# An attention and expert block: the values product of a group in one run, and a router with the experts held still in four column quarters

## The chip, the cores and the metric

The kernel runs on one core of a Trainium2 chip. The metric is the device time of one execution in microseconds (us). A core has the engines TensorE (PE in the rows; its weight loads are PEld), VectorE (DVE), ScalarE (ACT), GpSimd (POOL) and SyncE (SP, which issues DMAs); each works through its own list of instructions in order, and they wait for each other by semaphores. PSUM has eight banks of 128 partitions x 512 float32.

## The reference

x is (16, 512, 1024), ctx (16, 512, 256). 16 heads of 64 are in 4 groups of 4; the heads of a group share one key and one value slice, and keys and values are both ctx.

```
scores = layernorm(x) @ ctx.T / 8, per head and its group's slice      # 512 x 512
out    = softmax(scores) @ v                                       # v = ctx
x      = x + out.reshape(b, s, 1024) @ Wc.T + bc
h      = layernorm(x)
logits = h @ gate_kernel                                           # 1024 -> 32 experts
top 8 of softmax(logits), renormalised
x      = x + sum over the 8 experts of weight * down(silu(gate(h)) * up(h))
```

## The kernel before, in words

One program does a setup (transposed output weights in a high and a low part), an attention stage (attention, projection, second layernorm, router, choice of experts and the table of their rows), a short schedule, and the experts stage. The change touches setup and attention only.

**The attention stage** goes over 64 tiles of 128 rows, four tiles (s = 0 to 3) to each of 16 batches b. The batches between the first and the last run in a hardware loop, four tiles to a pass, so each engine comes to the loop's end once per batch. Within a tile every engine runs over the heads h = 0 to 15 in the same way: `tile(t)` issues what is due at head h, in the order in which it is written. That order is fixed by hand in a set of dictionaries that name, for each kind of work, the heads at which it is issued. Work of several tiles is interleaved: while attention of tile i runs, the projection belongs to tile i-1, the second layernorm's transposes, router and choice to tile i-2, the ranks and table writes to tile i-3, and the first layernorm and queries to tile i+1.

**TensorE at head h of tile i**, in order: scores of head h+3 (lines 798 and 799, into one of two S banks; waits for the exponent of head h+1), the four transposes of the probabilities of head h (line 813), half a block of the values product at odd heads (line 836), key transposes for the next batch at four heads of tiles 3 and 0 (`KEYS`, line 785), the ranks at head 1 (lines 885, 886), chunks of the projection (`PROJECT`, line 855), the transposes of the second layernorm's rows at heads 4 and 5 (line 871), the router at head 6 (line 877), and a quarter of the next tile's query transposes at heads 10 to 13 (line 776; they all use one bank, so each waits until ScalarE has copied the one before, line 460).

**Values** (`values`, line 836). For a group of four heads, and each of four chunks c of 128 context rows, two products: the stationary operand is the value chunk, 128x64, and the moving one the transposed probabilities of two heads, 256 columns. The two go to column halves 0-63 and 64-127 of the array and to the partition halves of one O bank. A float32 product is two passes on the array. The block of a group (8 products, 16 passes) is issued in two halves: chunks 0 and 1 at the head 4g+1, chunks 2 and 3 at 4g+3, one group later than its probabilities.

**Projection** (`project`). A chunk c is three float32r products of 512 columns, with the stationary operands oT_hi, oT_hi and oT_lo. `PROJECT` maps a head to (back, n, c0, c1): half n of tile i-back, chunks c0 to c1. After an odd chunk of half n = 1 TensorE signals `out_read`, since oT_hi and oT_lo of that group may then be overwritten. The part that waits for it is not touched by the change:

```
OUT_NORM = {0: (1, 2), 4: (1, 3), 8: (0, 0), 12: (0, 1)}                          # L216
OUT_SPLIT = {h + 1: back_group for h, back_group in OUT_NORM.items()}
def split_out_hi(i, g):                                                           # ScalarE, L490
    act.wait_ge(onorm_ready, G * i + g + 1)
    if g < G - 1:
        wait(act, out_read, (G - 1) * (i - 1) + g + 1)
    act.activation(oT_hi[:, 2 * g:2 * g + 2, :], o_norm[:, :, :], ACT.Copy).then_inc(othi_ready, 1)
```

ScalarE issues it (line 496) at head 9 for group 0 of the running tile, and VectorE's `split_out_lo` (line 621) waits for it at the same head.

**ScalarE at head h**, in order: the copy of the transposed probabilities of head h (line 487; VectorE has those of heads 1, 5, 9, 13, line 607), the exponent of head h+3 (line 479), `split_out_hi`, values and keys of the next batch (`keys_hi`, lines 471, 472), `normalise2` at head 3 (line 502), copies of its transposes at 4 and 5 (line 509), `normalise1` of the next tile at 6 (line 448), the high part of its queries at 7 (line 455), `top_exponent` at 8 (line 515), query copies at 10 to 13.

**VectorE at head h**: the maximum of head h+3 (line 592), inverses at 2, 6, 10, 14, its probability copies, the output's normalisation and low part, ranks at 2, statistics at 1, 2, 11 and 15, the table entries at 3 and 5, the logits and the choice of experts at 7, halves of the residual at 8 and 15. **POOL**: both layernorms' factors, the low part of the queries (line 393) at head 7, the bias addition (line 399) at 8, and eight table scatters (line 411).

**Router** (`router`, line 877): for each of eight chunks of 128 features, xn2T[:, c] (128x128) is stationary and gate_sb[:, c] (128x32) moves; all eight add up in one bank. VectorE copies the 32 logits of each row at head 7, and the second half of the projection, which uses the same bank, waits for that copy.

Of the kernel before, what the change touches and what calls it, by code (L numbers as in the profile page):

```python
# [16 lines left out]
F32 = mybir.dt.float32  # L17
# [7 lines left out]
P = 128  # L25
# [31 lines left out]
def moe_block(nc, x, ctx_in, Wc, bc, gate_w, gate_proj, up_proj, down_proj, out):  # L57
# [36 lines left out]
    with top:  # L94
        def sb(ctx, name, shape, dt):
            return ctx.enter_context(nc.sbuf_tensor(name, shape, dt))
# [11 lines left out]
        with attention_mem:  # L108
# [4 lines left out]
            ones_bf = sb(attention_mem, "ones_bf", [P, P], BF16)  # L113
            gate_sb = sb(attention_mem, "gate_sb", [P, DC, E], F32)
            bias_row = sb(attention_mem, "bias_row", [P, D], F32)
            iota_e = sb(attention_mem, "iota_e", [P, E], F32)
            token_id = sb(attention_mem, "token_id", [P, 1], F32)

            setup_stage(nc, sb, sem, banks, Wc, bc, gate_w, xn_dram, table, out, ident, ident_r, before_bf,
                        ones_bf, gate_sb, bias_row, iota_e, token_id, slot_base, expert_base, WcT_hi, WcT_lo,  # L120
                        D=D, DC=DC, E=E, T=T, TABLE_ROWS=TABLE_ROWS)
# [31 lines left out]
            FACTOR_STEPS = 2 + 2 * NEWTON_STEPS  # L153
            ROOT_SEED = float(0x5f3759df)
            logits = sb(attention_mem, "logits", [P, E], F32)
            top_v = sb(attention_mem, "top_v", [P, TOP_K], F32)
# [40 lines left out]
            ln2_chain = sem("ln2_chain")  # L197
            pool2_chain, ln2_ready, xn2_ready = sem("pool2_chain"), sem("ln2_ready"), sem("xn2_ready")
            xt2_done, xt2_copied, router_done, logits_copied = sem("xt2_done"), sem("xt2_copied"), sem("router_done"), sem("logits_copied")
            top_ready, topexp_ready, chosen_ready, rank_done = sem("top_ready"), sem("topexp_ready"), sem("chosen_ready"), sem("rank_done")  # L200
            rank_copied, entry_ready = sem("rank_copied"), sem("entry_ready")
            fence = {n: sem(f"fence_{n}") for n in ("dve", "pool", "sp")}

            BACK_STEPS = 12


# [11 lines left out]
            DVE_HEAD = 1  # L218
            VALUE_CHUNKS = {1: (0, 1), 3: (2, 3)}

            PROJECT = {0: (1, 0, 1, 2), 1: (1, 0, 2, 3), 2: (1, 0, 3, 4), 3: (1, 0, 4, 5), 4: (1, 0, 5, 6), 7: (1, 0, 6, 8),
                       8: (1, 1, 0, 2), 9: (1, 1, 2, 3), 10: (1, 1, 3, 4), 11: (1, 1, 4, 5), 12: (1, 1, 5, 6), 13: (1, 1, 6, 7),
                       14: (1, 1, 7, 8), 15: (0, 0, 0, 1)}
            NEXT_STATS, NEXT_FACTORS, NEXT_NORM, NEXT_SPLIT, NEXT_QUERIES, NEXT_BIAS = (1, 2), 2, 6, 7, (10, 11, 12, 13), 8
            RESIDUAL, STATS2 = (8, 15), (11, 15)
            FACTORS2, NORM2, TRANSPOSE2, ROUTER, CHOOSE, MARK, TOP_EXP = 0, 3, (4, 5), 6, 7, (11, 13), 8
            RANKS, TAKE_RANKS, PLACE, ENTER = 1, 2, 3, 5
# [216 lines left out]
            def _(act):  # L444
# [60 lines left out]
                def copy_xn2(j, n):  # L505
                    act.wait_ge(xt2_done, 2 * j + n + 1)
                    if n == 0:
                        wait(act, router_done, j)
                    act.activation(xn2T[:, 4 * n:4 * n + 4, :], turned(j, n)[:, :].rearrange("p (c t) -> p c t", c=4),
                                   ACT.Copy).then_inc(xt2_copied, 1)  # L510

                def top_exponent(j):
                    act.wait_ge(top_ready, j + 1)
                    wait(act, entry_ready, j)
                    act.activation(top_e[:, :], top_v[:, :], ACT.Exp, bias=neg_top[:, :], accum_out=top_s[:, :]
                                   ).then_inc(topexp_ready, 1)

                def tile(t):
                    i = t.i
                    for h in range(H):  # L520
# [14 lines left out]
                        if h in TRANSPOSE2 and t.back2:  # L535
                            copy_xn2(i - 2, TRANSPOSE2.index(h))
                        if h == NEXT_NORM and t.next:
                            normalise1(i + 1, t.next_s)
# [20 lines left out]
                for j in (LAST - 1, LAST):  # L559
                    normalise2(j)  # L560
                    for n in range(2):
                        copy_xn2(j, n)
                    top_exponent(j)

# [199 lines left out]
            def _(pe):  # L764
# [109 lines left out]
                def router(j):  # L874
                    pe.wait_ge(xt2_copied, 2 * j + 2)
                    for c in range(DC):
                        last = nc.tensor.matmul(turned(j, 0)[:, 0:E], xn2T[:, c, :], gate_sb[:, c, :], start=(c == 0), stop=(c == DC - 1))
                    last.then_inc(router_done, 1)

# [9 lines left out]
                def tile(t):  # L889
                    i = t.i  # L890
                    for h in range(H):
# [20 lines left out]
                        if h == ROUTER and t.back2:  # L912
                            router(i - 2)
                        if h in NEXT_QUERIES and t.next:
                            transpose_queries(i + 1, NEXT_QUERIES.index(h))
# [16 lines left out]
                for j in (LAST - 1, LAST):  # L932
                    for n in range(2):
                        transpose_xn2(j, n)
                    router(j)
                    ranks(j)

# [7 lines left out]

def setup_stage(nc, sb, sem, banks, Wc, bc, gate_w, xn_dram, table, out, ident, ident_r, before_bf, ones_bf, gate_sb,
                bias_row, iota_e, token_id, slot_base, expert_base, WcT_hi, WcT_lo, *, D, DC, E, T, TABLE_ROWS):
# [4 lines left out]
    with mem:  # L952
# [46 lines left out]
        def _(dve):  # L999
            dve.memset(zeros[:, :], 0.0).then_inc(empty_made, 1)  # L1000
            dve.memset(empty[:, :, 1], 0)
            dve.wait_ge(ident_made, 1)
            dve.tensor_copy(ident_r[:, :], ident[:, :]).then_inc(ident_r_made, 1)
            dve.wait_ge(made, 4)

# [654 lines left out]
```

## Time and profile before

| | us |
|---|---|
| median of 3 runs | 9428.77 (9426.17 to 9434.4) |
| the profiled execution | 9434.62 |
| its span, first to last instruction | 9432.9 |

| engine | busy us | share of the span |
|---|---|---|
| TensorE, products | 9123.3 | 97% |
| TensorE, weight loads | 7523.7 | 80% |
| VectorE | 5856.4 | 62% |
| POOL | 5063.9 | 54% |
| ScalarE | 4224.1 | 45% |

The shares are means over stages with different limits. The attention stage takes some 2669 us of the span, the experts stage nearly all the rest. Weight loads overlap with products, so the two lines of TensorE don't add up. The ends of products are modelled in the profile; distances between starts are the better measure of what one costs.

### The profile page before, as it was taken

How to read it: one execution, taken by the hardware profiler on the slowest of the kernel's cores; microseconds unless marked ns; L12 is line 12 of the kernel's file. 1: busy time of each engine (PE TensorE's matmuls, PEld its weight loads, DVE VectorE, ACT ScalarE, POOL GpSimd, SP SyncE). 2: the span in 40 equal slices, each digit the busy share in tenths (PEclk: the TensorE clock that was granted, in tenths of full speed). 3: DMA queues.
4: the chain of work that ended last, by engine and by line, in shares of the span. 5: the costliest groups of instructions: out<-in, count | busy, mean ns of one | idle time of the engine just before them, and what ended most of it. 6: DMA issues, size and time to landing. Idle time of an engine off the chain costs nothing.

```text
span 9432.9 us, 173987 instructions
## 1 busy us (share of the span) xinstructions
PE 9123.3 (97%) x46640; PEld 7523.7 (80%) x46641; DVE 5856.4 (62%) x9216; ACT 4224.1 (45%) x7010; POOL 5063.9 (54%) x4825
## 2 busy tenths in 40 slices
PE   8999999999969999999999999999999999999999
PEld 5777777777747888888888888888888888888888
DVE  5666666666645656666556666566666656656565
ACT  6666666666633333333333333333333333333333
POOL 2444444444445655666555566556665556555564
PEclk9999999999979999999999999999999999999999
DMA  2221212112124555555455555455555455555554
GB/s 96 60 57 59 63 53 63 57 55 64 56 62 106 119 109 113 115 128 127 107 108 110 111 133 119 105 113 113 114 117 119 106 125 107 119 107 111 125 115 81
DMA packets 723597, 926.17 MB, mean 98 GB/s; under 512 B 405521, under 2 KB 536593, under 8 KB 723090
## 3 DMA queue, kind: packets, MB, share of 16 engines
q0 software_dynamic: 209920, 604.72, 30.0%
q1 hardware_dynamic: 513298, 316.84, 13.0%
q8 instruction: 184, 3.01, 0.1%
q14 instruction: 195, 1.60, 0.1%
HBM read 1073.17 MB, written 376.45 MB: 154 GB/s over the span
## 4 chain that ended last, share of the span: by engine, by line
PE 61%; DMA 3%; issue 2%; DVE 2%; SPq 1%; ACT 1%; POOL 0%; DVEq 0%; ACTq 0%; POOLq 0%
PE bank L1569 40%; PE bank L1592 21%; DMA gu_raw<-in_L_ffn_up_proj 3%; SPq L1304 1%; DVE gu_lo L1483 0%; ACT xT_hi L1396 0%; ACT gu_hi L1403 0%; DVE xT L1472 0%; DVE h L1495 0%; DVE h_lo L1500 0%; DVE d_lo L1488 0%; DVE xT_lo L1477 0%; DVE h_hi L1498 0%; POOL xg L1356 0%; DVEq L41 0%
## 5 line engine op out<-in xcount | busy, mean ns | idle before, releaser
L1356 POOL DMA_INDIRECT xg<-xn_rows,gather_row x2304 | 2753.7, 1195 | 2076.9 <-PE bank L1569 1300.9
L1569 PE MATMUL bank<-xT_hi,gu_hi 128*128 128x512 f32 (+2 forms) x6912 | 2553.0, 369 | 106.4 <-DVE xT_lo L1477 95.9
L1569 PE MATMUL bank<-xT_lo,gu_hi 128*128 128x512 f32 (+2 forms) x6912 | 2543.1, 368 | 0.0
L1569 PE MATMUL bank<-xT_hi,gu_lo 128*128 128x512 f32 (+2 forms) x6912 | 2543.0, 368 | 0.0
L1414 ACT ACTIVATE gated<-bank 128x512 f32<-128x512 f32 x432 | 258.3, 598 | 3034.4 <-PE bank L1569 2681.5
L1569 PEld LDWEIGHTS bank<-xT_hi,gu_hi 128*128 128x128 f32 x6912 | 1299.1, 188 | 282.3 <-issue 94.9
L1368 POOL DMA_INDIRECT out_rows<-rows_out,entry_now x576 | 1139.0, 1977 | 678.3 <-DVE rows_out L1507 324.8
L1569 PEld LDWEIGHTS bank<-xT_lo,gu_hi 128*128 128x128 f32 x6912 | 1299.4, 188 | 159.3 <-issue 0.5
L1569 PEld LDWEIGHTS bank<-xT_hi,gu_lo 128*128 128x128 f32 x6912 | 1298.9, 188 | 158.8
L1592 PE MATMUL bank<-d_hi,h_hi 128*128 128x512 f32 x3162 | 1255.9, 397 | 70.1 <-DVE h_lo L1500 70.1
L1495 DVE TENSOR_TENSOR h<-bank,gated 128x512 f32<-128x512 f32 x432 | 297.6, 689 | 1580.9 <-ACT gated L1414 1195.1
L1592 PE MATMUL bank<-d_lo,h_hi 128*128 128x512 f32 x3162 | 1244.4, 394 | 0.0
L1592 PE MATMUL bank<-d_hi,h_lo 128*128 128x512 f32 x3162 | 1242.8, 393 | 0.0
L1483 DVE TENSOR_TENSOR gu_lo<-gu_raw,gu_hi 128x2048 fp32r<-128x2048 f32 x432 | 973.6, 2281 | 246.0 <-ACT gu_hi L1403 130.5
L592 DVE TENSOR_REDUCE neg_max<-bank 128x1 f32<-128x512 f32 x1024 | 704.4, 688 | 566.8 <-PE bank L799 464.2
L1403 ACT ACTIVATE gu_hi<-gu_raw 128x2048 fp32r<-128x2048 f32 x432 | 809.2, 1907 | 179.1 <-DMA gu_raw<-in_L_ffn_up_proj 165.4
L411 POOL DMA_INDIRECT slot_table<-entry,slot_i x512 | 507.9, 992 | 706.2 <-ACT pT L487 532.5
L479 ACT ACTIVATE probs<-bank,neg_max 128x512 f32<-128x512 f32 x1024 | 701.8, 685 | 344.1 <-DVE neg_max L592 307.4
L1507 DVE TENSOR_SCALAR rows_out<-bank,entry_now 128x512 f32<-128x512 f32 x576 | 431.3, 749 | 676.4 <-PE bank L1592 657.0
L1421 ACT ACTIVATE rows_out<-bank,entry_now 128x512 f32<-128x512 f32 x576 | 395.1, 686 | 1000.3 <-PE bank L1592 865.7
L1592 PEld LDWEIGHTS bank<-d_hi,h_hi 128*128 128x128 f32 x3162 | 600.8, 190 | 243.1 <-issue 122.6
L1472 DVE STREAM_TRANSPOSE xT<-xg 128x512 f32<-128x512 f32 x1152 | 747.3, 687 | 0.0
(159 smaller groups left out, 13150.0 us busy)
## 6 DMA issues: line engine op xcount, KB each, us to landing
gu_raw<-in_L_ffn_gate_proj SPq DMA_DIRECT2D x576, 384.0 KB
gu_raw<-in_L_ffn_up_proj SPq DMA_DIRECT2D x576, 384.0 KB
d_raw<-in_L_ffn_down_proj SPq DMA_DIRECT2D x144, 1536.0 KB
xg<-xn_rows,gather_row POOLq DMA_INDIRECT x2304
x_t<-in_x SPq DMA_DIRECT2D x64, 512.0 KB, 4.8
inv_wide<-inverse_sums SPq DMA_DIRECT2D x512, 64.0 KB
out_rows<-x SPq DMA_DIRECT2D x64, 512.0 KB, 5.5
xn_rows<-xn SPq DMA_DIRECT2D x64, 512.0 KB
```

The costliest lines, as they stand in the source:

```text
L411: pool.indirect_dma_start(out=table, out_offset=bass.IndirectOffsetOnAxis(ap=slot_i[:, k:k + 1], axis=0), in_=entry[:, k, :], in_offset=No ...
L479: act.activation(probs[h % 4][:, :], S_BANK[h % 2][:, :], ACT.Exp, bias=neg_max[:, h:h + 1], accum_out=row_sum[:, h:h + 1]).then_inc(exp_r ...
L592: dve.tensor_reduce(neg_max[:, h:h + 1], S_BANK[h % 2][:, :], AX.X, ALU.max, negate=True).then_inc(max_ready, 1)
L1356: pool.indirect_dma_start(out=xg[:, m, :], out_offset=None, in_=quarter_rows, in_offset=bass.IndirectOffsetOnAxis(ap=gather_row[:, m:m + 1 ...
L1368: pool.indirect_dma_start(out=out, out_offset=bass.IndirectOffsetOnAxis(ap=entry_now[:, q, 0:1], axis=0), in_=rows_out[:, q, :], in_offset ...
L1403: act.activation(gu_hi[:, :, :, cols], gu_raw[:, :, :, cols].rearrange("p n c m -> p c n m"), ACT.Copy).then_inc(guhi_ready, 1)
L1421: act.activation(rows_out[:, q, 0:512], D_BANK[q][0][:, :], ACT.Copy, scale=entry_now[:, q, 1:2].bitcast(F32)).then_inc(left_ready, 1)
L1472: dve.transpose(xT[:, :, 2 * pair * QUAD:2 * (pair + 1) * QUAD].rearrange("p c (m r) -> p m c r", r=QUAD), xg[:, 2 * pair:2 * pair + 2, :] ...
L1483: dve.tensor_tensor(gu_lo[:, :, :, cols], gu_raw[:, :, :, cols].rearrange("p n c m -> p c n m"), gu_hi[:, :, :, cols].bitcast(F32), ALU.su ...
L1507: dve.tensor_scalar(rows_out[:, q, 512:1024], D_BANK[q][1][:, :], entry_now[:, q, 1:2].bitcast(F32), None, ALU.mult).then_inc(right_ready, 1)
L1569: last = nc.tensor.matmul(bank[:, 0:cols], w[:, c, n, j * P:(j + 1) * P], v[:, c, 0:cols], start=(c == 0 and w is gu_hi and v is xT_hi), s ...
L1592: last = nc.tensor.matmul(D_BANK[q][n][:, 0:cols], v[:, k, q * P:(q + 1) * P], w[:, k, n * 512:n * 512 + cols], start=(k == ks[0] == 0 and ...
```

## The change

- The values block of a group is issued whole, at head 4g+1: `VALUE_CHUNKS` goes from {1: (0, 1), 3: (2, 3)} to {1: (0, 1, 2, 3)}.
- The chunks of the projection are laid on other heads, so that none shares a head with values.
- The router holds gate_sb[:, c] (128x32) still and moves xn2T[:, c] (128 columns). Chunk c goes to the column quarter c % 4, so that four partial sums of 32 experts x 128 rows stand in four partition quarters of a bank. ScalarE copies them (`copy_parts`, head 6), and one float32 product at head 7, with the copy stationary and a 128x32 matrix of ones in the right places moving (`fold`, made once in the setup), adds the quarters and turns the result back to rows x experts.

```diff
+            dve.tensor_reduce(fold[:, :], ident[:, :].rearrange("p (j e) -> p e j", e=E), AX.X, ALU.add)
...
-            VALUE_CHUNKS = {1: (0, 1), 3: (2, 3)}
-
-            PROJECT = {0: (1, 0, 1, 2), 1: (1, 0, 2, 3), 2: (1, 0, 3, 4), 3: (1, 0, 4, 5), 4: (1, 0, 5, 6), 7: (1, 0, 6, 8),
-                       8: (1, 1, 0, 2), 9: (1, 1, 2, 3), 10: (1, 1, 3, 4), 11: (1, 1, 4, 5), 12: (1, 1, 5, 6), 13: (1, 1, 6, 7),
-                       14: (1, 1, 7, 8), 15: (0, 0, 0, 1)}
+            VALUE_CHUNKS = {1: (0, 1, 2, 3)}
+
+            PROJECT = {0: (1, 0, 1, 2), 2: (1, 0, 2, 4), 3: (1, 0, 4, 5), 4: (1, 0, 5, 6), 6: (1, 0, 6, 7), 7: (1, 0, 7, 8),
+                       8: (1, 1, 0, 1), 10: (1, 1, 1, 3), 11: (1, 1, 3, 4), 12: (1, 1, 4, 6), 14: (1, 1, 6, 8), 15: (0, 0, 0, 1)}
...
-            FACTORS2, NORM2, TRANSPOSE2, ROUTER, CHOOSE, MARK, TOP_EXP = 0, 3, (4, 5), 6, 7, (11, 13), 8
+            FACTORS2, NORM2, TRANSPOSE2, ROUTER, FOLD, CHOOSE, MARK, TOP_EXP = 0, 3, (4, 5), 6, 7, 7, (11, 13), 8
...
+                def copy_parts(j):
+                    act.wait_ge(parts_done, j + 1)
+                    wait(act, router_done, j)
+                    act.activation(parts[:, :], turned(j, 0)[:, 0:P], ACT.Copy).then_inc(parts_copied, 1)
...
+                        if h == ROUTER and t.back2:
+                            copy_parts(i - 2)
                         if h == NEXT_NORM and t.next:
                             normalise1(i + 1, t.next_s)
...
                     for c in range(DC):
-                        last = nc.tensor.matmul(turned(j, 0)[:, 0:E], xn2T[:, c, :], gate_sb[:, c, :], start=(c == 0), stop=(c == DC - 1))
-                    last.then_inc(router_done, 1)
+                        rows = slice(E * (c % EXPERT_SETS), E * (c % EXPERT_SETS + 1))
+                        last = nc.tensor.matmul(turned(j, 0)[rows, 0:P], gate_sb[:, c, :], xn2T[:, c, :],
+                                                start=(c < EXPERT_SETS), stop=(c >= DC - EXPERT_SETS))
+                    last.then_inc(parts_done, 1)
+
+                def fold_parts(j):
+
+                    pe.wait_ge(parts_copied, j + 1)
+                    nc.tensor.matmul(turned(j, 0)[:, 0:E], parts[:, :], fold[:, :], start=True, stop=True).then_inc(router_done, 1)
...
+                        if h == FOLD and t.back2:
+                            fold_parts(i - 2)
```

## Rows read from the trace of the kernel before

**Rows 1.** The page, part 1: busy time of each engine over the whole span.
```profile
PE 9123.3 (97%) x46640; PEld 7523.7 (80%) x46641; DVE 5856.4 (62%) x9216; ACT 4224.1 (45%) x7010; POOL 5063.9 (54%) x4825
```

**Rows 2.** Windows: stretch, length, busy time (instructions) by engine, granted clock, DMA share, GB/s.
```profile
921.50:961.00 39.50, 39.50 (x251) 29.32 (x250) 26.10 (x61) 26.32 (x60) 18.18 (x31) 1.00 0.19 54
44.00:2713.00 2669.00, 2588.04 (x16210) 1912.32 (x16211) 1751.33 (x3932) 1774.21 (x3960) 1137.25 (x1879) 0.99 0.20 57
2217.10:2220.50 3.40, 3.40 (x13) 3.03 (x12) 2.14 (x6) 2.00 (x6) 0.00 (x0) 0.50 0.01 2
```

**Rows 3.** Timeline, a second tile, TensorE: start, length, instruction; heads 1 to 3.
```profile
921.51 0.39 PE L798 MATMUL bank<-kT,qT 128*128 128x512 f32 x1
...
922.50 1.08 PE L836 MATMUL bank<-pT,v 128*64 128x256 f32 x8
...
924.36 0.39 PE L798 MATMUL bank<-kT,qT 128*128 128x512 f32 x1
...
925.96 0.40 PE L798 MATMUL bank<-kT,qT 128*128 128x512 f32 x1
```

**Rows 4.** The same tile, TensorE: the router in head 6, and head 7.
```profile
934.23 1.91 PE L877 MATMUL bank<-gate_sb,xn2T 128*128 128x32 f32 x16
935.98 0.48 PE L798 MATMUL bank<-kT,qT 128*128 128x512 f32 x1
```

**Rows 5.** The same tile: a maximum in head 2, xn2, and its transposes in head 4.
```profile
925.02 0.69 DVE L592 TENSOR_REDUCE neg_max<-bank 128x1 f32<-128x512 f32 x1
...
928.95 1.23 ACT L502 ACTIVATE xn<-x,ln 128x1024 f32<-128x1024 f32 x1
...
930.38 0.60 PE L871 MATMUL bank<-ident,xn 128*128 128x128 f32 x4
```

**Rows 6.** The same tile: head 6 begins, normalise1, a short exponent, the bias addition.
```profile
933.24 0.48 PE L798 MATMUL bank<-kT,qT 128*128 128x512 f32 x1
...
936.13 1.23 ACT L448 ACTIVATE xn<-x_t,ln 128x1024 f32<-128x1024 f32 x1
...
941.86 0.30 ACT L515 ACTIVATE top_e<-top_v,neg_top 128x8 f32<-128x8 f32 x1
...
943.21 2.40 POOL L399 TENSOR_TENSOR x_t<-x_t,bias_row 128x1024 f32<-128x1024 f32 x1
```

**Rows 7.** The same tile: both splits, heads 10 and 11, the next head 1.
```profile
943.96 0.41 ACT L496 ACTIVATE oT_hi<-o_norm 128x256 fp32r<-128x256 f32 x1
...
944.40 1.50 DVE L621 TENSOR_TENSOR oT_lo<-o_norm,oT_hi 128x256 fp32r<-128x256 f32 x1 [0.55 <-ACT oT_hi L496]
...
944.71 0.39 PE L798 MATMUL bank<-kT,qT 128*128 128x512 f32 x1
...
945.83 0.68 DVE L592 TENSOR_REDUCE neg_max<-bank 128x1 f32<-128x512 f32 x1
...
947.22 0.59 ACT L460 ACTIVATE qT<-bank 128x512 fp32r<-128x512 f32 x1
...
949.48 0.46 PE L776 MATMUL bank<-ident_r,xq 128*128 128x128 f32 x4
...
961.02 0.39 PE L798 MATMUL bank<-kT,qT 128*128 128x512 f32 x1
```

**Rows 8.** Line 621 in this stage: count, ns min/median/max, first and last start, forms.
```profile
L621 DVE TENSOR_TENSOR oT_lo<-o_norm,oT_hi x252: 415/426/2703, 105.5 to 2699.2; 128x256 fp32r<-128x256 f32 x126
```

**Rows 9.** Timeline at a turn of a batch: head 14 begins; the standstill; head 2.
```profile
2203.38 0.47 PE L798 MATMUL bank<-kT,qT 128*128 128x512 f32 x1
...
2215.02 0.69 DVE L592 TENSOR_REDUCE neg_max<-bank 128x1 f32<-128x512 f32 x1 [4.88 <-issue]
...
2216.57 0.50 PE L798 MATMUL bank<-kT,qT 128*128 128x512 f32 x1 [2.98 <-ACT probs L479]
```

**Rows 10.** Timeline, a fourth tile, ScalarE: exponent of head 13, first query copy.
```profile
2194.56 0.69 ACT L479 ACTIVATE probs<-bank,neg_max 128x512 f32<-128x512 f32 x1 [0.16 <-DVE neg_max L592]
...
2196.46 0.60 ACT L460 ACTIVATE qT<-bank 128x512 fp32r<-128x512 f32 x1
```

More of the change, by code:

```diff
@@ L114, in moe_block @@
             gate_sb = sb(attention_mem, "gate_sb", [P, DC, E], F32)
+            fold = sb(attention_mem, "fold", [P, E], F32)
             bias_row = sb(attention_mem, "bias_row", [P, D], F32)
@@ L119, in moe_block @@
             setup_stage(nc, sb, sem, banks, Wc, bc, gate_w, xn_dram, table, out, ident, ident_r, before_bf,
-                        ones_bf, gate_sb, bias_row, iota_e, token_id, slot_base, expert_base, WcT_hi, WcT_lo,
+                        ones_bf, fold, gate_sb, bias_row, iota_e, token_id, slot_base, expert_base, WcT_hi, WcT_lo,
                         D=D, DC=DC, E=E, T=T, TABLE_ROWS=TABLE_ROWS)
@@ L154, in moe_block @@
             ROOT_SEED = float(0x5f3759df)
+            parts = sb(attention_mem, "parts", [P, P], F32)
             logits = sb(attention_mem, "logits", [P, E], F32)
@@ L198, in moe_block @@
             pool2_chain, ln2_ready, xn2_ready = sem("pool2_chain"), sem("ln2_ready"), sem("xn2_ready")
+            parts_done, parts_copied = sem("parts_done"), sem("parts_copied")
             xt2_done, xt2_copied, router_done, logits_copied = sem("xt2_done"), sem("xt2_copied"), sem("router_done"), sem("logits_copied")
@@ L204, in moe_block @@
             BACK_STEPS = 12
+            EXPERT_SETS = P // E
             AHEAD = 3
@@ L562, in _ @@
                         copy_xn2(j, n)
+                    copy_parts(j)
                     top_exponent(j)
@@ L935, in _ @@
                     router(j)
+                    fold_parts(j)
                     ranks(j)
@@ L943, in moe_block, with setup_stage @@
                       T=T, D=D, DC=DC, M=M, MC=MC, E=E, TABLE_PAD=TABLE_PAD, MOST_TILES=MOST_TILES, LEAST_TILES=LEAST_TILES)
-def setup_stage(nc, sb, sem, banks, Wc, bc, gate_w, xn_dram, table, out, ident, ident_r, before_bf, ones_bf, gate_sb,
+def setup_stage(nc, sb, sem, banks, Wc, bc, gate_w, xn_dram, table, out, ident, ident_r, before_bf, ones_bf, fold, gate_sb,
                 bias_row, iota_e, token_id, slot_base, expert_base, WcT_hi, WcT_lo, *, D, DC, E, T, TABLE_ROWS):
```

## The prediction

> **What bounds the kernel now.** I read the page first: TensorE is busy for 97% of the span, VectorE 62%, ScalarE 45% [rows 1]. The change touches only the attention stage, so I took that stage by itself: 2669 us, with TensorE busy for 2588 of them [rows 2]. It works through 64 tiles of 128 rows, 16 heads each, four tiles to a batch. In the second and third tile of a batch TensorE has no idle time at all: 39.5 of 39.5 us, against 26.1 for VectorE and 26.3 for ScalarE [rows 2]. At the turn of a batch it waits, 2.98 us for an exponent in the one shown; there VectorE sat for 4.88 us with "issue" named, waiting for nothing that the profile shows [rows 9]. So every microsecond taken from TensorE counts in the second to fourth tile, as long as no other engine becomes late. The timeline of one second tile is for finding that out. I count its times from the start of a head (its line 798 product); head h issues the scores of head h+3.
>
> **Values in one block: what TensorE saves.** Head 1 holds half a block, two rank products and one chunk of the projection, and lasts 924.36 - 921.51 = 2.85 us; head 2, without the half block, lasts 1.60 [rows 3]. Less 0.07 for the ranks, half a block costs about 1.2. Its 8 passes go in pairs; the pairs are (1.08 - 0.40)/3, about 0.22, apart (0.40 for the last pass itself is an estimate from the 0.39 of a score product), so four more pairs add 0.88. Two halves are 2.4, one whole 2.1: 0.35 saved per group, 1.4 per tile. It is the bracket around a block that goes. A chunk of the projection is 0.70: head 2 with one lasts 1.60, head 6 without one 2.74 less its router's 1.75, 0.99, of which 0.1 is a slower start behind the xn2 transposes [rows 3, 4, 6]. The Trainium skill ("TensorEngine Tiling (Array Packing)", Key Properties) has it that a switch of tiling mode drains the engine; by that rule one bracket in two goes, as the rows have it.
>
> **Router: what TensorE saves.** Now 16 passes last 935.98 - 934.23 = 1.75 us, 0.11 each [rows 4]. No row shows four column quarters at once. If they overlap as the two halves of the values do, four steps of 128 columns at 0.11 remain, plus a bracket of 0.3: 0.75. If they don't overlap at all, it is 1.75 + 0.3 = 2.05. I take 0.75, the nearer row being the values'. The fold is two more passes, 0.22. ScalarE gains a copy of 128x128, between its 0.30 for 8 columns and its 1.23 for 1024 [rows 5, 6]; I take 0.35, the near end, 0.25 of it before the next instruction starts. Saved on TensorE: 1.75 - 0.75 - 0.22 = 0.8 per tile. The Trainium skill ("TensorE: Matmul & The Clock Gate", Part 3) measured three column tiles at 2.38 times, not 3; by it the router would take some 0.1 longer, 6 us over the kernel, which the range holds.
> Both savings together: 64 x 1.4 + 62 x 0.8 = 139 us (the last two routers run behind the loop, beside table writes). The fold matrix is one reduction under the weight load of the setup: nothing.
>
> **Where it is taken back, stretch by stretch in a second tile** (A = start of head 1).
> *Head 1 to the transposes of xn2 in head 4.* Now they start at A + 8.87 (930.38 - 921.51), 0.20 after ScalarE has finished xn2 (928.95 + 1.23) [rows 3, 5]. The order is VectorE's: the maximum at 925.02 follows the scores that head 2 begins with, then come inverses, ranks and statistics, the next maximum, the exponent and xn2, done 5.16 later. After: head 1 has the whole block and no chunk, 2.93; head 2 two chunks, 2.40; head 3 none of the block, 1.60; TensorE arrives at A + 8.53. But the maximum comes 0.17 later, so xn2 can be turned at A + 8.90. Nothing is gained here; 0.37 of waiting is new.
> *To head 6.* Head 5 has the whole block, 0.88 more: 3.72 instead of 2.86 (933.24 - 930.38) [rows 5, 6].
> *Head 6 to head 10.* Now 944.71 - 933.24 = 11.47 [rows 6, 7]. After: head 6 a chunk and the router, 2.35; head 7 a chunk and the fold, 1.85; head 8 a chunk, 1.68; head 9 the whole block, 2.88: 8.76. The fold waits for nothing: ScalarE copies the parts at head 6 + 2.5 to 2.75, the fold comes at 4.05. It holds VectorE's choice of experts back until head 7 + 3.1, so the maximum of head 11 slips by 0.7; its exponent is needed two heads later.
> *Head 10 to 11: a new wait.* split_out_hi of group 0 (ScalarE, head 9) waits out_read, which the second half's chunk 1 of the tile before gives. That chunk sat in head 8; PROJECT now has it in head 10. ScalarE does its work in order, and VectorE's split_out_lo waits behind it in VectorE's order. Counted from head 10: the last product of chunk 1 begins at 1.47 (a bare head, 0.9 to 1.0, and two products of a chunk) and ends 0.40 later, so ScalarE's split starts at 1.93 (now at -0.75) and VectorE's at 2.37 (now at -0.31) [rows 7]. Now that VectorE instruction takes 1.50 instead of its median 0.43 [rows 7, 8], since POOL's bias addition runs from 943.21 to 945.61 and it ends 0.29 behind that [rows 6]. Where does POOL stand after? Its addition ends 9.48 behind the start of normalise1 (945.61 - 936.13), and that comes 2.73 into head 6 (now 2.89; the copy of the parts is ahead of it): head 6 + 12.21, that is head 10 + 3.45, from + 1.05. VectorE is caught again and is free at 3.74. The maximum of head 13 starts at 3.67, the copy of the first queries 1.39 behind it (947.22 - 945.83), at 5.06, done 5.65. The second query transposes of head 11 need that copy (one bank): 5.70. TensorE would be there at 4.39 and waits 1.3. The Trainium skill ("SBUF — State Buffer", Terms) says that the port pair VectorE and GpSimd share is held for a whole instruction; the 1.50 us agree, and by this rule the first rival below can't come by the split not being held.
> *From there to the next A.* Now 961.02 - 949.48 = 11.54 [rows 7]; after one chunk more, 0.70, and one bracket less, -0.36: 11.88.
> Sum: 8.90 + 3.72 + 8.76 + 5.70 + 11.88 = 38.96 against 39.51 now. Of 2.2 us saved, 0.55 is left.
>
> **The other tiles.** In the fourth tile of a batch keys_hi stands between the exponent of head 13 and the query copy, 1.9 us from exponent to copy instead of 0.68 [rows 10]. That is hidden now; after, it is on the new chain: + 1.2, less 0.43 for the key transposes that are no longer waited behind, and xn2 has no slack there now. I get + 0.8 for this tile up to head 14. From there to the next batch's fifth scores 13.19 us pass now (2216.57 - 2203.38), ended by VectorE's standstill [rows 9], which hangs on the key transposes of head 14 and not on what moves; and on to xn2 VectorE is the late one. TensorE's savings there turn into idle. The first tile, behind its xn2, gains its router and loses to keys_hi in head 6 and a later POOL: -0.15. A batch: -0.15 - 0.55 - 0.55 + 0.8 = -0.45; over 15.5 batches -7 us.
> **The clock.** The stage's mean granted clock is 0.99, the steady tiles' 1.00; behind the 2.98 us wait it was 0.50 for 3.4 us, that is 1.2 instead of 2.4 GHz [rows 2, 9]. Such a stretch costs up to 1.7 us. The new waits of 1.3 to 2.1 us may call some more: I add 3 us.
> The profiled run took 9434.6 us (span 9432.9), 5.9 above the median of 9428.8. 9434.6 - 7 + 3 = 9430.6; less 5.9: **9425 us**.
>
> **Rivals.**
> - *The out_read wait is there, POOL isn't in the way* (the addition ends before head 10 + 2.4, or the split isn't held). VectorE is free at 2.8, the second transposes start at 4.75, 0.95 less in 62 tiles: 9366. For it: POOL's place rests on a sum of ten terms. Against: it is caught with a microsecond to spare on both sides.
> - *Everything TensorE saves is kept* but the 0.37 at xn2: 9429 - 139 + 23 = 9313. For it: 97% busy, the other engines at two thirds in this stage. Against: the two waits above are written in the code.
> - *Slower: the quarters don't overlap.* The router ends 12 x 0.11 = 1.3 us later, and all of it is on the chain from head 6 over the parts, normalise1 and POOL to head 11: 62 x 1.3 = 81, 9506. It decides from 0.75 + 0.1 + 0.3 us of router on. Against: the halves overlap.
> - *The clock falls in every second new wait* of the two tiles per batch with 2 us: some 20 to 50 us more, 9445 to 9475. The 2.98 wait speaks for it; against it, these are shorter.
>
> **Chances.** Forecast 0.45 (own range 9400 to 9450), POOL not in the way 0.17, all kept 0.10, no overlap 0.08, clock 0.15, else 0.05. I call "same" what is within 0.2%, 19 us, about what a measurement of this kernel can tell. Of the forecast's own 0.45, 0.10 lies below, 0.30 within, 0.05 above; with the rivals: faster 0.38, same 0.34, slower 0.28. Range 9355 to 9475: it leaves out all kept and no overlap.
>
> **What would show it.** The block of values at 16 passes and about 1.9 us; the router line at well under 1 us; a second tile near 39.0 us, not 37.3; ScalarE's line 496 in head 9 waiting for line 855 and starting 1.9 behind head 10; line 621 there again at 1.4 and not 0.43; idle of about 1.3 ahead of line 776 in head 11, ended by ScalarE's qT; a new idle of 0.4 ahead of line 871. If there is no idle ahead of 776, the forecast is wrong on its main step; if the router line still shows 1.7, on the price of the quarters.

## Result and the profile after

The changed kernel takes 9460.6 us (median of 10 runs, 9448.8 to 9476.7) against 9435.1 for the kernel before in the same session (10 runs, 9426.2 to 9453.2): ratio 1.0025, 95% interval 1.0016 to 1.0033. It is slower by 0.25%. Of the cases in the prediction, the one that came true is the fourth rival, the clock, which had a chance of 0.15.

The profiled run took 9462.4 us (span 9460.6). First the page's busy times, which answer to [rows 1]:

```profile
PE 9037.1 (96%) x46768; PEld 7481.0 (79%) x46769; DVE 5831.9 (62%) x9217; ACT 4224.4 (45%) x7074; POOL 5066.2 (54%) x4825
```

TensorE is busy for 86 us less, and the span is 28 us longer: the work that was taken off has turned into waiting, and some more with it. (Busy time also holds what a low clock stretches, so the work saved is more than 86 us.) The windows say where (stretch, length, busy time of PE, PEld, DVE, ACT and POOL, granted clock, DMA share, GB/s): a second tile, the attention stage, and a stretch behind a wait in a fourth tile; they answer to [rows 2].

```profile
933.67:972.63 38.96, 37.63 (x253) 28.17 (x252) 25.66 (x61) 26.30 (x61) 18.43 (x30) 1.00 0.20 56
54.30:2715.90 2661.60, 2480.19 (x16194) 1853.73 (x16193) 1713.35 (x3901) 1760.49 (x3999) 1132.37 (x1860) 0.97 0.20 57
1210.60:1214.00 3.40, 3.40 (x11) 2.71 (x11) 2.33 (x5) 2.60 (x7) 1.16 (x2) 0.50 0.13 36
```

From the first to the last scores the stage takes 2661.6 us, and took 2636.9 before. A second tile takes 38.96, as forecast, but it now holds 1.3 us of idle time. The stage's mean clock is 0.97 and was 0.99.

The timeline of that second tile (start, length, engine, line, operation, count, idle time before it and what ended it) answers to [rows 3 to 7]. Line 809 opens a head.

```profile
933.67 0.39 PE L809 MATMUL bank<-kT,qT 128*128 128x512 f32 x1
...
934.65 1.95 PE L847 MATMUL bank<-pT,v 128*64 128x256 f32 x16
...
941.28 1.23 ACT L505 ACTIVATE xn<-x,ln 128x1024 f32<-128x1024 f32 x1
...
942.57 0.66 PE L882 MATMUL bank<-ident,xn 128*128 128x128 f32 x4 [0.22 <-ACT xn L505]
...
946.34 0.48 PE L809 MATMUL bank<-kT,qT 128*128 128x512 f32 x1
...
948.10 0.64 PE L889 MATMUL bank<-xn2T,gate_sb 128*32 128x128 f32 x16
...
948.67 0.50 PE L809 MATMUL bank<-kT,qT 128*128 128x512 f32 x1
948.81 0.28 ACT L518 ACTIVATE parts<-bank 128x128 f32<-128x128 f32 x1
948.99 1.23 ACT L451 ACTIVATE xn<-x_t,ln 128x1024 f32<-128x1024 f32 x1
...
950.38 0.30 PE L896 MATMUL bank<-fold,parts 128*128 128x32 f32 x2
...
955.07 0.50 PE L809 MATMUL bank<-kT,qT 128*128 128x512 f32 x1
...
956.04 2.42 POOL L402 TENSOR_TENSOR x_t<-x_t,bias_row 128x1024 f32<-128x1024 f32 x1
...
956.96 0.42 ACT L499 ACTIVATE oT_hi<-o_norm 128x256 fp32r<-128x256 f32 x1 [2.00 <-PE bank L866]
...
957.41 1.34 DVE L632 TENSOR_TENSOR oT_lo<-o_norm,oT_hi 128x256 fp32r<-128x256 f32 x1 [2.66 <-ACT oT_hi L499]
...
960.07 0.59 ACT L463 ACTIVATE qT<-bank 128x512 fp32r<-128x512 f32 x1
...
960.71 0.54 PE L787 MATMUL bank<-ident_r,xq 128*128 128x128 f32 x4 [1.11 <-issue]
...
972.63 0.39 PE L809 MATMUL bank<-kT,qT 128*128 128x512 f32 x1
```

The reader is to see two things. The parts are cheaper than before: the router runs from 948.10 to the next head at 948.67, 0.57 us for 16 passes where it was 1.75; a block of values takes 1.95. And in head 10 (955.07) three instructions are late one behind the other: ScalarE's split, which waited for the projection (line 866); VectorE's split, which takes 1.34 us, until 0.29 behind the end of GpSimd's addition; and then the query copy, for which TensorE waits 1.11 us at line 787.

The fourth tile, TensorE in heads 11 and 12, is where the forecast ends:

```profile
1210.04 0.54 PE L787 MATMUL bank<-ident_r,xq 128*128 128x128 f32 x4 [1.91 <-ACT qT L463]
1210.42 0.60 PE L809 MATMUL bank<-kT,qT 128*128 128x512 f32 x1
1210.82 0.63 PE L810 MATMUL bank<-kT_swapped,qT 128*128 128x512 f32 x1
...
1214.67 0.47 PE L809 MATMUL bank<-kT,qT 128*128 128x512 f32 x1
```

Head 12 lasts 1214.67 - 1210.42 = 4.25 us. Where the clock stays up it lasts 2.65. The difference, some 1.6, stands in 12 of the 14 fourth tiles from the second batch on.

Below, "half-clock time" is the time in the attention stage at a granted clock of 0.50, that is 1.2 GHz in place of 2.4, summed from the clock's record in the trace: 49.8 us before, 139.1 us in the changed kernel. 6 to 9 us of each such sum belong to a stretch that had begun before the stage did. All others begin in a first or a fourth tile of a batch; none begins in a second or third.

### The profile page after: what moved, and what is told of

The parts are those of the page before. It is cut to its first block, busy times and chain, and to the rows that moved or that the text cites. A ratio compares the mean times of both kernels' runs of the same rounds, so it can differ in the third digit from the quotient of the medians.

```text
span 9460.6 us, 174371 instructions
## 1 busy us (share of the span) xinstructions
PE 9037.1 (96%) x46768; PEld 7481.0 (79%) x46769; DVE 5831.9 (62%) x9217; ACT 4224.4 (45%) x7074; POOL 5066.2 (54%) x4825
## 4 chain that ended last, share of the span: by engine, by line
PE 63%; issue 2%; DMA 2%; DVE 1%; ACT 1%; SPq 0%; POOL 0%; DVEq 0%; ACTq 0%; POOLq 0%
PE bank L1591 41%; PE bank L1614 22%; DMA gu_raw<-in_L_ffn_up_proj 2%; ACT xT_hi L1418 0%; SPq L1326 0%; DVE gu_lo L1505 0%; DVE xT L1494 0%; DVE h L1517 0%; DVE xT_lo L1499 0%; ACT gu_hi L1425 0%; DVE d_lo L1510 0%; DVE h_lo L1522 0%; DVE h_hi L1520 0%; POOL xg L1378 0%; DVEq L41 0%
```

## Experiments

All were timed in five rounds beside the kernel before (the ratio is to that), with one profile each. The first four went together, then three, then three. Tile times are means over the twelve batches 3 to 14 (heads 1 to 14 of a fourth tile run from the start of head 1 to the start of head 14); stage and half-clock time are those of the one profiled execution.

| kernel | median us | ratio, 95% interval | stage us | second tile | fourth tile, heads 1 to 14 | half-clock us |
|---|---|---|---|---|---|---|
| before | 9435 to 9441 | 1 | 2636.9 | 39.51 | 33.95 | 49.8 |
| changed | 9460.6 | 1.0025 (1.0016 to 1.0033) | 2661.6 | 38.98 | 36.25 | 139.1 |
| E1 chunk 1 back | 9422.7 | 0.9981 (0.9972 to 0.9990) | 2613.6 | 39.00 | 35.21 | 90.1 |
| E2 router alone | 9391.1 | 0.9951 (0.9937 to 0.9965) | 2588.3 | 38.60 | 33.39 | 51.2 |
| E3 values alone | 9484.1 | 1.0050 (1.0036 to 1.0064) | 2675.0 | 39.81 | 36.39 | 85.6 |
| E4 addition late | 9384.1 | 0.9945 (0.9931 to 0.9958) | 2577.6 | 38.07 | 34.35 | 69.5 |
| E5 E1 and E4 | 9347.3 | 0.9904 (0.9889 to 0.9919) | 2540.2 | 37.62 | 32.87 | 70.8 |
| E6 before, addition late | 9439.1 | 1.0000 (0.9991 to 1.0009) | 2641.5 | 39.51 | 33.94 | 57.9 |
| E7 changed, head 11 filled | 9448.7 | 1.0006 (0.9997 to 1.0015) | 2646.8 | 39.00 | 34.82 | 97.3 |
| E8 changed, three waits filled | 9428.4 | 0.9992 (0.9983 to 1.0001) | 2626.7 | 38.99 | 34.81 | 39.0 |
| E9 before, two waits filled | 9426.4 | 0.9988 (0.9979 to 0.9997) | 2633.0 | 39.51 | 33.94 | 8.2 |
| E10 E5, two waits filled | 9330.1 | 0.9887 (0.9872 to 0.9902) | 2534.4 | 37.61 | 32.88 | 12.0 |

### E1: chunk 1 of the second half back in head 8

```
-  8: (1, 1, 0, 1), 10: (1, 1, 1, 3)
+  8: (1, 1, 0, 2), 10: (1, 1, 2, 3)
```

> The changed kernel with one chunk of the projection put back: chunk 1 of the second half in head 8 and not in head 10 (head 10 keeps chunk 2). Theory A (the loss comes through the wait on out_read: directly by the late split in head 11, and by the low clock that follows such waits in the fourth tile): ScalarE's split in head 9 and VectorE's in head 10 wait for nothing, VectorE's takes 0.43 us and not 1.34, no idle of 1.1 us ahead of the second query transposes of head 11, second tile 37.7 us (38.98 less 1.1 to 1.3), the idle in the fourth tile gone, and the time at half clock in the stage down from 139 us towards 50; together some 110 us less than the changed kernel, 9350. Rival B (the loss has nothing to do with out_read; the mode changes of the quarters or the block cost more than their rows show): within 20 us of the changed kernel, 9460. Between them, 9390 to 9410, if only the waits go and the clock stays as it is.

None of the three: 9422.7, with the second tile unchanged at 39.00. The wait on out_read is gone, and nothing came of it there. The timeline of E1 in heads 9 to 11 shows why:

```profile
936.61 0.40 ACT L499 ACTIVATE oT_hi<-o_norm 128x256 fp32r<-128x256 f32 x1
936.70 1.00 POOL L414 DMA_INDIRECT slot_table<-entry,slot_i  x1 [0.16 <-issue]
937.05 3.37 DVE L632 TENSOR_TENSOR oT_lo<-o_norm,oT_hi 128x256 fp32r<-128x256 f32 x1 [0.55 <-ACT oT_hi L499]
...
937.72 2.41 POOL L402 TENSOR_TENSOR x_t<-x_t,bias_row 128x1024 f32<-128x1024 f32 x1
...
942.37 0.54 PE L787 MATMUL bank<-ident_r,xq 128*128 128x128 f32 x4 [1.14 <-ACT qT L463]
```

VectorE's split now begins 2.0 us earlier, counted from the start of head 6 (at 9.08 in place of 11.09), and ends where it did (12.45 and 12.43), that is 0.29 behind the end of GpSimd's addition (937.72 + 2.41 = 940.13; 937.05 + 3.37 = 940.42). It lasts 3.37 us in place of 0.43. It begins 0.67 before the addition's record does, 0.35 into a table write of GpSimd. My theory A had this wrong: I had taken the wait on out_read for the cause, and it was only one of two. What the edit did give, 0.44% or some 40 us, came in the first and fourth tiles, with 49 us less at half clock.

### E2: the new router alone

The router, its fold and its copy as changed; the placing as before:

```
- VALUE_CHUNKS = {1: (0, 1, 2, 3)}
+ VALUE_CHUNKS = {1: (0, 1), 3: (2, 3)}
+ PROJECT = ...   # the kernel before's
```

> The changed kernel's router in quarters with its fold, but the values in two half blocks and the projection's chunks as before the change. Theory A: the router gives what its rows show, 1.75 - 0.64 - 0.14 = 0.9 us per tile less some slack, no new wait on out_read, second tile 38.7 us against 39.5, and the clock as in the kernel before: 50 us less than before, 9385. Rival B (the quarters cost as much as they save): within 20 us of before, 9435. Rival C (the fold's chain over ScalarE's copy delays VectorE's choice of experts and with it the fourth tile): slower than before.

Theory A: 9391.1, second tile 38.60, 0.91 below before, and no more half-clock time than before (51.2). The quarters overlap: head 6 with the router lasts 1.65 us in place of 2.74. The fold adds 0.14 to head 7 and no wait to a second tile. So the router's gain arrives there when nothing else moves; a fourth tile up to head 14 gains less, 0.56 us (33.95 to 33.39).

### E3: the values in one block alone

The counterpart, in the kernel before:

```
- VALUE_CHUNKS = {1: (0, 1), 3: (2, 3)}
+ VALUE_CHUNKS = {1: (0, 1, 2, 3)}
+ PROJECT = ...   # the changed kernel's
```

> The router as before the change (16 passes on one bank, no fold), but the values in one block and the changed placing of the projection's chunks. Theory A: the out_read wait of 2 us at ScalarE's split in head 9 and the idle ahead of the second query transposes of head 11 are there without the new router; the second tile is about 39.0 to 39.6 us, the fourth tile has its stall and half-clock stretches as in the changed kernel: 9440 to 9480, no faster than before. Rival B (the router is what costs): 9350 to 9390, faster than before by the block's 0.35 us per group.

Theory A, at the far end of it: 9484.1, 0.5% slower than before, second tile 39.81. The same late row of instructions as above, without the new router (in this kernel's own line numbers):

```profile
958.64 2.43 POOL L398 TENSOR_TENSOR x_t<-x_t,bias_row 128x1024 f32<-128x1024 f32 x1
...
959.57 0.42 ACT L495 ACTIVATE oT_hi<-o_norm 128x256 fp32r<-128x256 f32 x1 [2.47 <-PE bank L854]
...
960.02 1.33 DVE L620 TENSOR_TENSOR oT_lo<-o_norm,oT_hi 128x256 fp32r<-128x256 f32 x1 [3.14 <-ACT oT_hi L495]
...
963.31 0.53 PE L775 MATMUL bank<-ident_r,xq 128*128 128x128 f32 x4 [1.10 <-ACT qT L459]
```

So the whole loss comes with the block and the placing of chunks that goes with it. A wait of 1.9 us at line 775 stands in its fourth tiles as well, and head 12 is a slow one in 6 of 14.

### E4: GpSimd's bias addition in head 12 in place of 8

```
- NEXT_BIAS = 8
+ NEXT_BIAS = 12
```

> The changed kernel with GpSimd's addition of the bias row issued four heads later (head 12 and not 8). The wait on out_read stays; only the addition that holds VectorE's split is moved out of its way. Theory A: ScalarE's split still waits 2 us for the second product of chunk 1, VectorE's split takes 0.43 us and not 1.34, the idle ahead of the second query transposes of head 11 falls from 1.1 to about 0.3 us, second tile 38.1 us, some 55 us less than the changed kernel by the direct way, and fewer half-clock stretches in the fourth tile: 9385 to 9405. Rival B (the split isn't held by the addition, or the bias's later users become late): no shorter than the changed kernel, 9460.

Theory A, 0.9 us below its 9385 to 9405: 9384.1, second tile 38.07, the wait on out_read as long as ever, the split at 0.42 and 0.22 us of idle left at line 787.

```profile
928.03 0.42 ACT L499 ACTIVATE oT_hi<-o_norm 128x256 fp32r<-128x256 f32 x1 [2.00 <-PE bank L866]
...
928.48 0.42 DVE L632 TENSOR_TENSOR oT_lo<-o_norm,oT_hi 128x256 fp32r<-128x256 f32 x1 [2.67 <-issue]
...
930.86 0.54 PE L787 MATMUL bank<-ident_r,xq 128*128 128x128 f32 x4 [0.22 <-ACT qT L463]
```

This is the prediction's first rival made real (the out_read wait there, GpSimd not in the way: 0.95 less in a second tile). It is 0.91.

### E5: both edits

E1's line of PROJECT and E4's NEXT_BIAS in the changed kernel.

> The changed kernel with both edits: chunk 1 of the second half back in head 8, and GpSimd's bias addition issued in head 12. Theory A2 (either of the two, the wait on out_read or the hold by GpSimd's addition, is enough by itself to make the first queries' copy late in head 11; with chunk 1 back the split starts 0.35 us into a table write of GpSimd that the addition follows, and is held 3.37 us to the addition's end, in place of 0.43): with neither, VectorE's split takes 0.43 us although it still starts inside a table write, no idle ahead of the second query transposes, second tile 37.8 us; half-clock time in the stage near 50 us; 9365. Rival D (the table write itself holds the split): the split still takes 1 us or more, second tile above 38.3, 9390 or more.

Theory A2, and more than it asked for: 9347.3, 0.96% faster than before. The second tile is 37.62 and its wait at line 787 is gone:

```profile
913.09 1.00 POOL L414 DMA_INDIRECT slot_table<-entry,slot_i  x1
913.44 0.42 DVE L632 TENSOR_TENSOR oT_lo<-o_norm,oT_hi 128x256 fp32r<-128x256 f32 x1 [0.55 <-ACT oT_hi L499]
...
917.47 0.46 PE L787 MATMUL bank<-ident_r,xq 128*128 128x128 f32 x4
```

The split begins 0.35 into the same table write as in E1 and takes 0.42. So it isn't the table write that holds it (rival D), it is the addition queued behind the write. Half-clock time is 70.8, more than the 50 I expected; all of the stretches begin in first tiles. The result lies 18 us below the 9365 I had written, so that sum had the gain too small.

### E6: the later addition in the kernel before

E4's edit, NEXT_BIAS 12 in place of 8, in the kernel before.

> The kernel before, with GpSimd's bias addition issued in head 12 and not 8; a control. Theory A2: its held split (1.50 us) is off the path there, so the second tile stays at 39.51 us with the split at 0.43, and the time is that of before within 15 us, 9438. Rival E (a later addition pays by itself, whatever the placing of the chunks): 20 us or more below before.

Ratio 1.0000. The second tile stays at 39.51 to the hundredth, while the split in its head 9 takes 0.42 us at the median of 16 tiles and took 1.50; no split lasts longer than 1.6 us (line 621: count, ns min/median/max; it answers to [rows 8], where the longest was 2703):

```profile
L621 DVE TENSOR_TENSOR oT_lo<-o_norm,oT_hi x256: 415/425/1567, 82.6 to 2707.0; 128x256 fp32r<-128x256 f32 x128
```

The hold of 1.50 us was there all along and cost nothing; in the changed placing the same hold costs 0.9 us a tile.

### E7: the fourth tile's wait filled with unused products

```
+ if h == 11 and t.s == SC - 1 and t.next:
+     pe.wait_ge(pt_by_act, by_act(i, 10))
+     for _ in range(6):
+         nc.tensor.matmul(PT_BANK[0][:, :], WcT_hi[:, 0, 0:P], WcT_hi[:, 0, 0:HALF], start=True, stop=True)
```

> The changed kernel with six products of 128x512 (1.4 us) on data that is not used, in head 11 of each fourth tile, into a bank whose content has been read and is written anew in head 12. They fill most of the wait of 1.9 us ahead of the second query transposes and change nothing else. Clock theory (head 12 of the fourth tile lasts 4.24 us and not 2.65 because the clock is granted at half after that wait): head 12 there is 2.65 us again, the fourth tile falls by 1.4 us on the mean, half-clock time in the stage falls from 139 us to some 90, and the kernel gains 20 to 30 us although TensorE has more to do: 9435. Rival (the 1.6 us are a wait or contention of another kind): head 12 stays at 4.2 us, the time at 9460.

```profile
1034.02 1.55 PE L937 MATMUL bank<-WcT_hi 128*128 128x512 f32 x6
1036.08 0.54 PE L787 MATMUL bank<-ident_r,xq 128*128 128x128 f32 x4 [0.52 <-ACT qT L463]
...
1036.45 0.46 PE L809 MATMUL bank<-kT,qT 128*128 128x512 f32 x1
...
1039.11 0.46 PE L809 MATMUL bank<-kT,qT 128*128 128x512 f32 x1
```

The clock theory holds: head 12 is 2.65 to 2.67 us, in every fourth tile, none of the stretches begins in a fourth tile any more, and that tile falls from 36.25 to 34.82. The query copy comes no earlier; TensorE has six more products to do, and the kernel is 0.19% faster for them (1.0025 to 1.0006), about 18 us. I had written 20 to 30.

### E8 and E9: the long waits of the first tile filled too, after and before

```
+ if h == 1 and t.s == 0: unused_products(0, by_act(i, 0), 8)
+ if h == 4 and t.s == 0: unused_products(1, by_act(i, 3), 10)   # ahead of the transposes of xn2
```

`unused_products(bank, copied, n)` is E7's edit as a function: it waits until that bank has been copied and issues n such products into it. E8 has these two and E7's; E9 is the kernel before with these two.

> The changed kernel with unused products of 128x512 in the three places of a batch where TensorE waits longest: 8 at the end of head 1 and 10 ahead of the transposes of xn2 in head 4 of the first tile, 6 ahead of the second query transposes in head 11 of the fourth (the last as in the run before). Clock theory: half-clock time in the stage falls from 139 us to 30 or less, the waits stay where they are (second tile 38.98, fourth tile 34.8), and the stage falls by 0.35 us for each us of it, to 2620 us; together with the kernel before under the same products the forecast's sum without the clock can be read: -0.45 us per batch and -7 us in all would make it 2615 to 2625 against before's. Rival (the low clock has another source than these waits, or the unused products make other things late): half-clock time above 80 us.

> The kernel before with the same unused products in the first tile of each batch (8 at the end of head 1, 10 ahead of the transposes of xn2 in head 4); a control. Clock theory: half-clock time from 50 us to 20 or less, the stage some 10 us shorter, 9425. The difference between this run and the changed kernel with its products is what the change does with the clock taken out: my forecast has -7 us, a cost of the kind 'mode changes and waits cost more than the rows show' would leave +15 us or more.

The windows of the two stages, E8's first:

```profile
54.80:2681.40 2626.60, 2523.44 (x16572) 1894.84 (x16570) 1707.51 (x3901) 1757.90 (x3999) 1132.20 (x1860) 0.99 0.20 58
```

```profile
55.00:2687.90 2632.90, 2610.03 (x16361) 1934.86 (x16360) 1737.49 (x3902) 1761.61 (x3939) 1123.21 (x1861) 1.00 0.20 57
```

With the waits filled, the stage of the changed kernel is 6.3 us shorter than that of the kernel before; my sum without the clock was -7. The medians are 9428.4 and 9426.4, with overlapping intervals: no difference. (The profiled execution of E8 lies 5.7 us below the median of its runs, that of E9 at its median, so the 6.3 is a soft number.) E8 still has 39.0 us at half clock against 8.2, eight of its nine stretches in head 12 of the first tile, where there is a wait that I didn't fill. All of E9's 8.2 belong to the stretch that began ahead of the stage. That is more than the 30 I expected. E9's stage fell by 3.9 us where I had some 10, its median by 11.

### E10: E5 with the first tile's waits filled

> The best version so far (chunk 1 back in head 8, bias addition in head 12) with the unused products of the first tile. Clock theory: half-clock time from 71 us to 25 or less, 15 to 20 us less than that version: 9330. Rival (a product that isn't used costs as much as it gives): 9347 or more.

The clock theory: 9330.1 us, 1.1% faster than before (ratio 0.9887, 0.9872 to 0.9902), half-clock time 12.0. It is the best version measured, though its interval overlaps with E5's. Its third tiles take 38.56 us against 37.61 for a second, and took 38.01 in E5. In head 10 of a third tile VectorE waits for the inverses of the softmax sums to come back from memory; whether that makes the tile late, and why it is later than in E5, was not tried.

```profile
951.17 0.42 DVE L627 TENSOR_TENSOR o_norm<-bank,inv_wide 128x256 f32<-128x256 f32 x1 [2.81 <-DMA inv_wide<-inverse_sums]
```

## Why the prediction was wrong

The forecast was 9425, the result 9460.6. It lies inside the range, and the sign is wrong. By the prediction's own steps:

- *Savings on TensorE.* Router: 0.75 forecast; 0.57 measured from its first pass to the next head, and in E2 0.09 more ahead of it (its first pass comes 0.20 behind the pass before, where it came 0.11). Fold: 0.22 forecast, 0.14 measured; head 7 is 1.84, forecast 1.85. Block of values: 1.95, forecast "about 1.9". E2 and E5 show them arrive: 0.91 us per second tile for the router (forecast 0.8), and 38.60 - 37.62 = 0.98 for the block (1.4, less the 0.37 at xn2). Right.
- *The second tile.* 38.98 measured, 38.96 forecast. The agreement isn't luck: leg by leg the rows give 8.90, 3.77, 8.73, 5.64 and 11.92 against 8.90, 3.72, 8.76, 5.70 and 11.88. The transposes of xn2 come 8.90 behind the start of head 1, as forecast, with a wait ahead of them (the row says 0.22). ScalarE's split starts 1.89 behind head 10 (1.93), VectorE's lasts until 3.68 (3.74), the second query transposes start at 5.64 (5.70) behind 1.11 of idle (1.3). Right, with the cause that was given for it. E1 and E4 add what the sum didn't say: two waits end at nearly the same moment here. Taking away out_read's gives nothing (39.00), taking away the addition's gives 0.91, both give 1.36. The forecast named them in the right order, and its rival put the right price on the second.
- *The fourth tile up to head 14.* +0.8 forecast. With the clock up it is 34.81 - 33.94 = +0.87 (E8 against E9). Right. As it ran it is +2.30, and the 1.4 in between is the clock.
- *Turn of the batch and first tile.* Forecast 0 and -0.15. Measured in the filled pair (E8 against E9): from head 14 to the next head 2 11.84 against 12.81, -0.97. That comes with the block and its placing: the same stretch is 12.86 in E2 and 11.95 in E3, 12.84 before; what shortens it wasn't tried. From the xn2 transposes to the next head 1 it is 32.04 against 31.10, +0.94, and that is the clock: head 12 is half-clocked in 7 of the 12 batches of E8, which take 32.69 here, and the other five take 31.14, +0.04. The turn was off, by about 1 us. The batch is 165.99 against 166.22, -0.23; in the five batches whose head 12 keeps its clock it is 165.31, -0.9. Forecast -0.45, so without the clock the change gives about twice what was forecast, some 14 us (an estimate: 15.5 x 0.9).
- *The clock.* This is the step that failed: "The new waits of 1.3 to 2.1 us may call some more: I add 3 us". Half-clock time went from 49.8 to 139.1 us. Filling the waits takes 0.33% off the changed kernel (1.0025 to 0.9992, 31 us) and 0.12% off the kernel before (11 us), so as far as the filling reaches, the clock cost the change 20 us more than it cost the kernel before, and E8 still holds 31 us more half-clock time than E9. At 0.35 us for each us of it (E8 against the changed kernel in the stage: 34.9 for 100.1) that is another 11, an estimate: 31 together. By the batch times of the profiles it is 37: 168.45 in the changed kernel against 165.31 where the clock stays up, 166.98 in the kernel before against 166.22 in E9, a difference of 2.38 over 15.5 batches. So the term is some 30 to 40 us and not 3, and it turns a gain into a loss: the -14 above and this +37 are the +23 by which 15.5 batches of the two kernels differ, and their medians differ by 25. The fourth rival priced it at 20 to 50 and gave it 0.15; it expected a fall at every second new wait, and in the fourth tiles it was 12 of 14.

Why it was sized at 3: there was one example in front of me, a wait of 2.98 us [rows 9], and the new waits were shorter, so I expected few falls. The trace of before had 18 waits of over 2.2 us in this stage, 11 of them with a half-clock stretch at them; it had only four between 1.7 and 2.2, one with such a stretch. In the changed kernel there are again 18 of over 2.2, now 16 with a stretch, and 32 between 1.7 and 2.2, 18 with one: most of the added half-clock time stands at those. The fourth tile's wait was forecast as one of "the two tiles per batch with 2 us", and a price of up to 1.7 us for each was in reach (1.6 as measured): 15 x 1.6 = 24 us, more than three times the gain of 7 that was forecast. A forecast of -7 that rests on the difference of large terms should have had the clock as a term of its own, with its count.

Left open: why the same wait brings the clock down in one kernel and not in another. Head 11 of the fourth tile takes 4.1 us in the changed kernel and in E1, with a wait of 1.9 us ahead of line 787 in each of 14 tiles; a slow head 12 follows in 12 of them in the one and in 4 in the other (in 6 in E3, with the same wait). And why a VectorE instruction is held 0.67 us before the record of GpSimd's addition begins (E1). GpSimd's spans are rough; whether the hold starts earlier than the record or the record is late wasn't tried.

## What to carry to other kernels

When work is taken off an engine that is never idle, list each wait that then shows and price it twice: its length, and the slow clock that may come behind it (here up to 1.6 us, at 1 of 262 waits under 1.7 us and at 180 of 290 longer ones); where waits recur once per batch, the second price can exceed the whole saving. Two waits that end together hide each other: removing the one that the profile names may give nothing (E1) until the other goes too (E5), so try both together before giving up on either. And keep the placing of a part apart from the part: the router alone gave 0.49%, the block in its placing took 0.50%, and the same block with one chunk and one addition moved made the whole 0.96%.

## What the runs showed of the hardware

- Four column quarters overlap: 16 passes of 128 columns into four sets of 32 partitions take 0.57 us from the first pass to the next instruction on the whole array, against 1.75 for 16 passes of 32 columns one after the other. The first pass comes 0.20 us behind the pass ahead of it, in place of 0.11 (E2).
- A VectorE instruction that reads two operands from SBUF (the split, 128x256, 0.43 us by itself) lasts until 0.29 us behind the end of a GpSimd addition of two SBUF operands: 1.34, 1.33 and 3.37 us in three kernels. The Trainium skill ("SBUF — State Buffer", Terms) says that the two engines share a port pair that is held for a whole instruction; that agrees. VectorE's instructions that read a bank of PSUM kept their time beside the same additions: in the kernel before, 0.68 us for 17 copies of 128x512, where the others take 0.68, and 0.43 us for 7 normalisations of the output, where the others take 0.42.
- It was held even where, by the records, it began inside a table write and 0.67 us ahead of the addition that followed (E1, 3.37, in 31 tiles), and not where the write was followed by another write (E5, 0.42).
- The clock fell behind long waits of TensorE and by no means each time. Over the attention stage in the twelve profiles of this case, counted from 0.2 us ahead of a wait to 3.5 us behind it, a half-clock stretch began at 1 of 262 waits of 0.9 to 1.7 us, at 47 of 119 of 1.7 to 2.2, and at 133 of 171 above that. Of the 181 stretches 163 took 3.4 us and 18 took 6.8; TensorE's work ran slower in them (a head of 2.65 us lasted 4.25).
- Products that nobody reads, put into such waits, were worth 0.12% to the kernel before, 0.33% to the changed one and some 0.2% to the best (there the intervals overlap).
